# Between shared expert and routed experts: the tables, the zero rows and the first weights set up inside the shared expert's last chunk

## The reference: what is computed

```python
h = layernorm(x) * (1 + cb) + sb
scores = sigmoid(h @ router_weight.T)                 # 4096 tokens, 16 experts
idx = grouped top-2 of (scores + e_bias)              # 4 groups of 4, 2 groups kept
w = scores at idx, divided by their sum
routed = sum over the 2 chosen e: w_e * (relu2(h @ w_up[e]) @ w_down[e])   # 512 -> 256 -> 512
shared = relu2(h @ shared_up) @ shared_down                                # 512 -> 1024 -> 512
out = x + gb * (routed + shared)
```

## Time and profile before

| | before |
|---|---|
| time, median of 3 runs | 2291.51 us (2287.38 to 2297.24) |
| the profiled execution: its own time | 2298.3 us |
| its span in the trace | 2296.4 us |
| PE busy | 1909.7 us, 83% |
| DVE busy | 1264.3 us, 55% |
| ACT busy | 822.5 us, 36% |
| POOL busy | 687.5 us, 30% |
| shared stage's last chunk, from PE's first up matmul's relu to the last add | about 1809 to 1855 us of the span |

### The profile page before, as it was taken

The page is one execution under the profiler, slowest core; times in us unless marked ns, Lnnn a source line. Parts: engine busy times, 40 slices in busy tenths (PEclk is TensorE's granted clock), DMA queues, the critical chain, the costliest instruction groups (busy, mean ns, idle before and its releaser), DMA issues. The chain is left out here.

```text
span 2296.4 us, 34896 instructions
## 1 busy us (share of the span) xinstructions
PE 1909.7 (83%) x9947; PEld 1197.6 (52%) x9948; DVE 1264.3 (55%) x3069; ACT 822.5 (36%) x1372; POOL 687.5 (30%) x775
## 2 busy tenths in 40 slices
PE   4789989899899999899899885999999928999900
PEld 0645434644435644436544433777777727888800
DVE  3356657345566355573565627555555336575558
ACT  1335445245453254452344522222222104545400
POOL 0101116001124011143011243445545569260064
PEclk8789999899999899999899996999999969999955
DMA  6221131222312222404112314222222157554388
GB/s 217 60 45 36 42 101 61 61 56 56 75 37 67 54 56 56 111 6 115 29 38 45 74 65 143 92 87 91 87 91 88 70 193 258 189 183 153 135 307 319
DMA packets 104960, 232.37 MB, mean 101 GB/s; under 512 B 20440, under 2 KB 20440, under 8 KB 104812
## 3 DMA queue, kind: packets, MB, share of 16 engines
q1 hardware_dynamic: 81008, 171.86, 25.8%
q0 software_dynamic: 14848, 50.34, 6.3%
q10 hardware_dynamic: 8960, 8.41, 1.2%
HBM read 113.06 MB, written 67.17 MB: 78 GB/s over the span
## 5 line engine op out<-in xcount | busy, mean ns | idle before, releaser
L400 ACT ACTIVATE pr<-sc 128x1024 f32<-128x1024 f32 (+3 forms) x384 | 308.1, 811 | 320.1 <-PE sc L669 286.0
L324 POOL TENSOR_SCALAR_AFFINE_SELECT pr<-pr 128x256 f32<-128x256 f32 x256 | 105.7, 413 | 1008.8 <-ACT pr L400 1008.6
L689 PE MATMUL O<-pr,V 128*32 128x512 f32 (+3 forms) x3072 | 339.7, 518 | 13.3 <-ACT oD L412 13.2
L513 DVE TENSOR_REDUCE mx<-ring 128x1 f32<-128x512 f32 x256 | 169.6, 679 | 282.7 <-PE ring L644 281.6
L509 DVE CUSTOM_DVE_ANT_0 ring<-ring,mask 128x512 f32<-128x512 f32 (+3 forms) x512 | 240.9, 512 | 81.0 <-PE ring L644 80.0
L669 PE MATMUL sc<-stk 128*128 128x512 f32 (+3 forms) x768 | 251.6, 410 | 19.6 <-ACT pr L400 17.6
L669 PEld LDWEIGHTS sc<-stk 128*128 128x128 f32 x768 | 120.4, 196 | 268.0 <-ACT pr L400 154.0
L644 PE MATMUL ring<-stk 96*128 96x512 f32 (+3 forms) x768 | 225.5, 393 | 39.0 <-DMA stk<-st 28.5
L644 PEld LDWEIGHTS ring<-stk 96*128 96x128 f32 x768 | 147.6, 208 | 92.0 <-issue 25.0
L538 DVE RECIPROCAL oD<-oD 128x128 f32<-128x128 f32 x128 | 117.7, 935 | 32.9 <-ACT oD L412 32.9
L635 PE MATMUL ring<-hhi,whi 128*128 128x512 f32 x256 | 111.4, 435 | 27.2 <-DVE hlo L488 15.2
(11 more groups left out here) (246 smaller groups left out, 3776.5 us busy)
## 6 DMA issues: line engine op xcount, KB each, us to landing
stk<-st SPq DMA_DIRECT2D x192, 256.0 KB, 5.1
x_e<-xs SPq DMA_DIRECT2D x79, 256.0 KB, 2.6
ys<-y_e SPq DMA_DIRECT2D x79, 256.0 KB, 2.0
xt<-in_L_attn_x_dram ACTq DMA_DIRECT2D x16, 512.0 KB, 5.5
st<-in_L_attn_x_dram SPq DMA_DIRECT2D x32, 256.0 KB, 2.7
x1d<-pr SPq DMA_DIRECT2D x32, 256.0 KB, 2.0
xb<-x1d SPq DMA_DIRECT2D x32, 256.0 KB, 3.0
part<-y_sh SPq DMA_DIRECT2D x32, 256.0 KB, 2.0
```

The costliest lines, as they stand in the source:

```text
L324: nc.gpsimd.affine_select(out=t, in_=t, compare_op=ALU.is_ge, fill=0.0, base=0, pattern=[[0, 2], [1, P]], channel_multiplier=-1).then_inc( ...
L400: nc.scalar.activation(pr[:, g % PRB, :, off:], sc[g % 2][:, :, off:], ACT.Exp, scale=SCALE).then_inc(exp_done, 1)
L513: nc.vector.tensor_reduce(mx[:, heads[0]:heads[-1] + 1, qt, part], bank[:, 0:len(heads) * w].rearrange("p (e k) -> p e k", e=len(heads)), ...
L689: last = nc.tensor.matmul(O[row:row + 32, off:], V[:, col:col + DH], pr[:, g % PRB, e, off:], start=(i == 0), stop=(i == 4 * c + 3))
```

## The change

What stood at the start of `expert_phase` moves into the last chunk of `shared_phase` (`b is None`). DVE makes the tables in four pieces behind the squares of blocks 2 to 5 (`count_tiles`, `place_tiles`, `find_tiles`, `list_tiles`), and copies them and works out `K.rows` between the second and the third `scaled` (`copy_tables`, `move_rows`). PE's three small transposes stand behind `down(q, 0)`. SP issues the 16 zero-row DMAs ahead of the last chunk's four stores, and waits for them at the end of the stage. POOL fetches experts 0, 1 and 2 ahead of its low parts 1, 2 and 3; ahead of its first two adds it splits experts 0 and 1, and ahead of the other two it fetches experts 3 and 4. `expert_phase` starts with the loads of x and with expert 2's split. The new tensors lie in memory that is dead by then: the weight slots over `uphi`, `uplo` and the other parity's `xb` and `h2`, the raw buffers over `dn_own` and the other parity's half of `turned`, which now holds `thi` and `tlo` together; the tables' scratch is `bc[:, 0]`. The iotas move to the start of the shared stage.

```diff
+def fetch_weights(nc, K, e): ...
+def split_high(nc, K, e): ...
+def split_low(nc, K, e): ...
-        xb = sb("xb", [P, 2, TPC, D])
-        h2 = sb("h2", [P, 2, TPC, D])
+        xb, h2 = [None, None], [None, None]
+        for par in range(2):
+            xb[par], h2[par] = sb(f"xb{par}", [P, TPC, D]), sb(f"h2_{par}", [P, TPC, D])
+        ahi = sb("ahi", [P, FC, CH], f32r)
+        alo = sb("alo", [P, FC, CH], f32r)
+        dn_own = sb("dn_own", [P, FC - 2, D])
+        turned = sb("turned", [P, 2, 2, KC, CH], f32r)
+        thi, tlo = turned[:, :, 0, :, :], turned[:, :, 1, :, :]
...
 # SP, chunk
+                if not more and q == NCH - 1:
+                    sp.wait_ge(pads_known, 1)
+                    for e in range(E):
+                        row = sp.value_load(K.padi[0:1, e:e + 1], min_val=e * REGION, max_val=e * REGION + T)
+                        sp.dma_start(K.xs[bass.ds(row, P), :], zero[:, :]).then_inc(padded, 16)
...
             sp.wait_ge(zero_out, 16)
+            sp.wait_ge(padded, 16 * E)
...
 # POOL, chunk
                 for m in range(FC):
+                    if b is None and 1 <= m <= RAW:
+                        fetch_weights(nc, K, m - 1)
                     low(q, m)
...
                 for j in range(TPC):
+                    if b is None and j < EARLY:
+                        pool.wait_ge(K.raw_in[j], 32)
+                        split_high(nc, K, j)
+                        split_low(nc, K, j)
+                    if b is None and EARLY <= j < 2 * EARLY:
+                        pool.wait_ge(K.w_ready, 2 * (j - EARLY) + 2)
+                        fetch_weights(nc, K, j - EARLY + RAW)
...
 # DVE, chunk
+                    if b is None and m == 2:
+                        count_tiles()
+                    if b is None and m == 3:
+                        place_tiles()
+                    if b is None and m == 4:
+                        find_tiles()
+                    if b is None and m == 5:
+                        list_tiles()
...
                 scaled(q, par, 1)
+                if b is None:
+                    copy_tables()
+                    move_rows()
                 scaled(q, par, 2)
...
 # PE, chunk
+                else:
+                    pe.wait_ge(in_columns, 1)
+                    for n in range(3):
+                        last = nc.tensor.transpose(tp[0][0:1, n, 0:NET], rowf[0:NET, 2 + n:3 + n], K.ident[0:NET, 0:NET])
+                    last.then_inc(in_rows, 1)
                 down(q, 1, range(FC // 2))
...
+EARLY = 2
...
 # expert_phase, SP
-            sp.wait_ge(tables, 1)
-            sp.wait_ge(zeroed, 1)
-            for e in range(E):
-                row = sp.value_load(padi[0:1, e:e + 1], min_val=e * REGION, max_val=e * REGION + T)
-                sp.dma_start(K.xs[bass.ds(row, P), :], zero[:, :]).then_inc(padded, 16)
-            sp.wait_ge(padded, 16 * E)
...
 # expert_phase, POOL
-            for e in range(RAW):
-                fetch(e)
-            for e in range(E):
-                if e == WR:
-                    pool.wait_ge(tables, 1)
-                split(e)
-                if e + RAW < E:
-                    pool.wait_ge(w_ready, 2 * e + 2)
-                    fetch(e + RAW)
+            for e in range(EARLY, E):
+                pool.wait_ge(K.raw_in[e % RAW], (e // RAW + 1) * 32)
+                split_high(nc, K, e)
+                split_low(nc, K, e)
+                if e + RAW < E:
+                    pool.wait_ge(K.w_ready, 2 * e + 2)
+                    fetch_weights(nc, K, e + RAW)
```

More of the change, by code:

```diff
@@ L843, in shared_phase @@
         y_out = [sem(f"y_out{i}") for i in range(2)]
+        K.rwhi = sb("rwhi", [P, KC, E], f32r)
+        K.rwlo = sb("rwlo", [P, KC, E], f32r)
+        K.ebias = sb("ebias", [P, E])
+        K.order = sb("order", [P, E])
+        K.region = sb("region", [P, E])
+        K.gtri = sb("gtri", [P, NG, NG])
+        K.tri = sb("tri", [P, P], bf16)
+        K.ones = sb("ones", [P, P], bf16)
+        kf, jf, ef = sb("kf", [P, NTILE]), sb("jf", [P, 1]), sb("ef", [P, E])
+        k_i, j_i, e_i = (sq[:, 0, at:at + n].bitcast(mybir.dt.int32) for at, n in ((0, NTILE), (NTILE, 1), (2 * NTILE, E)))
+        scratch = bc[:, 0, :, :].rearrange("p a d -> p (a d)")
+        more = scratch[:, 0:E * NTILE].rearrange("p (e k) -> p e k", k=NTILE)
+        mine = scratch[:, 0:2 * NTILE * E].rearrange("p (n e) -> p n e", e=E)
+        own = scratch[:, 2 * NTILE * E:]
+        ntile, ones_e, ends, starts, base, inside, other, padf, order_e, shift, rowf = (own[:, n * E:(n + 1) * E] for n in range(11))
+        moved = own[:, 11 * E:11 * E + 2 * NTILE]
         rw_raw = relu[0:E, 0, :]
         zero = sb("zero", [P, D])
-        dn_own = sb("dn_own", [P, FC - 2, D])
-        up_raw = [(slice(0, 2), xb[:, 1, :, :].rearrange("p j d -> p (j d)").rearrange("p (k n) -> p k n", k=2)),
-                  (slice(2, 4), h2[:, 1, :, :].rearrange("p j d -> p (j d)").rearrange("p (k n) -> p k n", k=2))]
+        up_raw = [(slice(0, 2), xb[1][:, :, :].rearrange("p j d -> p (j d)").rearrange("p (k n) -> p k n", k=2)),
+                  (slice(2, 4), h2[1][:, :, :].rearrange("p j d -> p (j d)").rearrange("p (k n) -> p k n", k=2))]
         dn_raw = [(slice(0, FC - 2), dn_own[:, :, :]), (slice(FC - 2, FC), y[:, :, :])]
@@ new lines, in place_tiles, with find_tiles @@
+            def place_tiles():
+                table(nc.vector.tensor_tensor_scan(ends, ones_e, ntile, 0.0, ALU.mult, ALU.add))
+                table(tt(starts, ends, ntile, ALU.subtract))
+                table(ts(base, starts, -float(P), -float(DUMMY), ALU.mult, ALU.add))
+                table(nc.vector.scalar_tensor_tensor(base, ef[:, :], float(REGION), base, ALU.mult, ALU.add))
+                nc.vector.tensor_scalar(K.endi[:, :], ends, float(PRIMED), None, ALU.add)
+            def find_tiles():
+                ts(inside, starts, jf[:, 0:1], None, ALU.is_le)
+                table(ts(other, ends, jf[:, 0:1], None, ALU.is_le))
+                table(tt(inside, inside, other, ALU.subtract))
+                red(rowf[:, 2:3], other, AX.X, ALU.add)
+                table(red(rowf[:, 0:1], inside, AX.X, ALU.add))
+                table(ts(rowf[:, 2:3], rowf[:, 2:3], float(E - 1), None, ALU.min))
+                table(tt(other, inside, base, ALU.mult))
@@ L1197, in transposes @@
                 for k in range(KC):
-                    last = nc.tensor.transpose(tp[j % 2][:, k, :], h2[:, par, j, k * P:(k + 1) * P], K.ident[:, :])
+                    last = nc.tensor.transpose(tp[j % 2][:, k, :], h2[par][:, j, k * P:(k + 1) * P], K.ident[:, :])
                 last.then_inc(t_done, 1)
@@ L1535, in _ @@
-            nc.vector.tensor_copy(jf[:, :], j_i[:, :])
-            then(nc.vector.tensor_copy(ef[:, :], e_i[:, :]))
-            then(tt(more[:, :, :], K.count[:, :].unsqueeze(2).broadcast_to([P, E, NTILE]),
-                    kf[:, :].unsqueeze(1).broadcast_to([P, E, NTILE]), ALU.is_gt))
-            then(red(ntile[:, :], more[:, :, :], AX.X, ALU.add))
-            then(nc.vector.tensor_tensor_scan(ends[:, :], ones[:, :], ntile[:, :], 0.0, ALU.mult, ALU.add))
-            then(tt(starts[:, :], ends[:, :], ntile[:, :], ALU.subtract))
@@ L1551, in _ @@
-            ts(inside[:, :], starts[:, :], jf[:, 0:1], None, ALU.is_le)
-            then(ts(other[:, :], ends[:, :], jf[:, 0:1], None, ALU.is_le))
-            then(tt(inside[:, :], inside[:, :], other[:, :], ALU.subtract))
-            red(rowf[:, 2:3], other[:, :], AX.X, ALU.add)
-            then(red(rowf[:, 0:1], inside[:, :], AX.X, ALU.add))
-            then(ts(rowf[:, 2:3], rowf[:, 2:3], float(E - 1), None, ALU.min))
-            then(tt(other[:, :], inside[:, :], base[:, :], ALU.mult))
@@ L1586, in _ @@
         def _(pe):
-            pe.wait_ge(in_columns, 1)
-            for n in range(3):
-                last = nc.tensor.transpose(txb[0][0:1, n, 0:NET], rowf[0:NET, 2 + n:3 + n], K.ident[0:NET, 0:NET])
-            last.then_inc(in_rows, 1)
-            pe.wait_ge(tables, 1)
             slot = {}
```

209 lines of the change are left out of this document (98 added, 111 removed).

## The result

| | before | changed |
|---|---|---|
| time, median of 4 runs each, on one chip | 2294.38 us (2287.38 to 2301.44) | 2263.79 us (2255.4 to 2272.2) |
| ratio, with its 95% interval | | 0.9867 [0.9817, 0.9916] |
| the profiled execution's span | 2296.4 us | 2253.5 us |

What follows compares the result with a forecast made beforehand. PE's standstill between barrier and restart, 38.1 us, was taken as the passage to shorten. -33.0 + 6.8 = -26.2 us from the 2291.5 us median gave 2265 us; likeliest range 2259 to 2271, with the worse tail 2257 to 2274.

Steps and rivals of the forecast that it cites:

- The restart: Barrier to PE's restart: 5.1 us instead of 38.1, with 4.1 us for the load's landing; -33.0 us.
- The shared stage with its barrier: Shared stage's end: POOL's added work in the last chunk makes the last add end near 1862.0, +6.8 us.
- POOL's tail: Last chunk: two splits, four adds and two fetches take 22.3 us, plus 1.5 us lost to DVE.
- The sends' end: Last chunk: low part 7 and the sends end perhaps 0.5 us later, 1838.2 instead of 1837.7.
- The chunks ahead: Shared stage before the last chunk: iotas and three copies at its start cost under 0.5 us, taken as 0.
- Add to barrier: Last add to barrier: stores come back within some 3 us; no added time counted.
- PE's down product: Last chunk: later by low part 7's 0.5 us plus about 0.6 us for three transposes, its end covered.
- The tables on DVE cost 0: Last chunk: squares may be late by 1 to 2 us, covered by POOL's lateness; cost 0, uncovered at most 2 us.
- Behind the restart: Expert stage: POOL has expert 3 split with 11 us to spare before tile 7 asks; taken as 0.

Runs made afterwards that it cites:

- b_zeros_late: Changed kernel, but SP stores the 16 rows of zeros behind the barrier again; 2293.13 us, ratio 0.9986 to the kernel before.
- a_layout: Kernel before with only the changed kernel's memory layout, no instruction moved; 2293.85 us, ratio 0.9994 to the kernel before.
- b_fetch_late: Changed kernel, but experts 3 and 4 are fetched behind the barrier; 2265.16 us, ratio 0.9868 to the kernel before.
- a_after: The changed kernel again, unchanged; 2266.24 us, ratio 0.9879 to the kernel before.
- c_best: Changed kernel, experts 0 and 1 split on ACT and DVE, experts 3 and 4 fetched earlier, row table later, sends behind low part 7; 2257.37 us, ratio 0.9819.
- d_final: c_best with three sends between low parts, five behind low part 7, experts 3 and 4 fetched behind the second add; 2257.82 us, ratio 0.9820 to before.
- b_no_weights: Changed kernel, but POOL fetches and splits no weights in the last chunk; 2268.75 us, ratio 0.9876 to the kernel before.
- a_before: The kernel before again, unchanged; 2295.86 us, ratio 0.9995 to itself.
- a_shift: Kernel before with only five small unused tensors put in front of the shared stage's memory; 2293.62 us, ratio 0.9989 to the kernel before.

## Why the prediction was right, and where only its sum was

**The restart, forecast -33.0 us, measured -34.8 us.** Barrier to restart went from 38.06 to 3.27 us. SP's first load is issued 0.8 us behind the barrier (1858.54, 1859.32), and PE starts 2.5 us after that. I had taken 4.1 us for this landing from the earlier trace rows; that load went out right behind 16 stores, and the median of the earlier trace rows, 2.6 us, was the better guide. b_zeros_late shows the mechanism: with the zeros back, the gain is gone.

**The shared stage with its barrier, forecast +6.8 us, measured +7.2 us (483.4 to 490.7), from other parts than I said.**
- POOL's tail from the last send to the last add: two splits, four adds and two fetches. Forecast 22.3 + 1.5 = 23.8 us; it took 23.5 us (from 1826.20, the last send's end, to 1848.39 + 1.28). Before it was 17.45 us. Of that, DVE cost 1.9 us (3.25 and 3.38 instead of 2.35 each), forecast 1.5.
- The sends' end: forecast 0.5 us late, measured 1.5 us, from the chunk's first `relu` (28.8 us before, 30.3 us now).
- The chunks ahead: the last one began 3.6 us earlier in the stage (at 431.65 and 428.05 us), which I had at zero. It lasts: in all ten profiles with the changed chunk it began at 425.0 to 428.2 us, in the four without it at 431.5 to 431.8. The layout's shorter blocks, 0.4 us in each of seven chunks, would be 2.8 us of it, but a_layout is one of the four, so what else is needed is open.
- Add to barrier: assumed unchanged at 5.57 us, measured 8.87 and 9.63 us. This step failed. I had reckoned the stores' landing "within some 3 us" and thought only of POOL's time for the fetches, not of their bytes ahead of the last stores. b_fetch_late shows it for 2.3 of the 3.3 us: 6.53 us without them.

So the forecast was 0 + 0.5 + 6.3 + 0 = 6.8, and the trace has -3.6 + 1.5 + 6.0 + 3.3 = 7.2. The two terms that I had at zero nearly cancel. That this sum came out right is therefore luck, not a forecast of its parts. Counted from the stage's start, the last add is 3.9 us later, not 6.8.

**"PE's down product ... its end is covered by what follows."** It was covered, but its size was wrong. I had put the low parts 0.5 us late. PE, with the clock in the stretches under the rows:

```profile
1820.15 0.50 PE L1414 MATMUL dn<-dnhi,ahi 128*128 128x512 f32 x1 [0.70 <-POOL alo L988]
1820.72 0.40 PE L1414 MATMUL dn<-dnhi,alo 128*128 128x512 f32 x1
1823.83 0.79 PE L1414 MATMUL dn<-dnhi,ahi 128*128 128x512 f32 x1 [2.71 <-POOL alo L988]
1824.43 0.63 PE L1414 MATMUL dn<-dnlo,ahi 128*128 128x512 f32 x1
1824.85 0.63 PE L1414 MATMUL dn<-dnhi,alo 128*128 128x512 f32 x1
...
1820.00:1822.00 2.00, 0.97 (x3) 0.48 (x3) 0.00 (x0) 0.00 (x0) 1.55 (x3) 1.00 1.02 395
1822.00:1824.00 2.00, 0.17 (x1) 0.17 (x2) 0.00 (x0) 0.00 (x0) 1.81 (x3) 0.66 1.01 383
1824.00:1826.00 2.00, 2.00 (x7) 1.50 (x8) 0.48 (x1) 0.00 (x0) 1.70 (x2) 0.50 0.88 335
1826.00:1828.00 2.00, 2.00 (x6) 1.52 (x6) 0.21 (x1) 0.00 (x0) 1.99 (x3) 0.50 0.91 344
1828.00:1830.00 2.00, 2.00 (x7) 1.59 (x6) 0.00 (x0) 0.00 (x0) 1.92 (x2) 0.64 0.72 270
1830.00:1832.00 2.00, 2.00 (x10) 1.68 (x9) 0.00 (x0) 0.00 (x0) 2.00 (x2) 1.00 0.25 93
```

PE waited 0.70 and 2.71 us for low parts 6 and 7, where before one wait of 1.40 us stood. Over the second its clock fell from 1.00 to 0.50, that is from 2.4 to 1.2 GHz, and from 1823.83 until 1829.2 its matmuls came 0.43 us apart instead of 0.227: 12 matmuls and three transposes, 5.7 us where some 3.1 would do, so 2.6 us. The last chunk took 48.1 us instead of 44.15 (48.4 in a_after): 2.0 from the waits, 2.6 from the clock, 0.3 to 0.6 from the transposes, less 1.3 us for 192 matmuls at the shorter pitch. It costs nothing in the changed kernel, since POOL's tail ends later still (5.7 us behind PE), but it is what c_best and d_final gain: there the down product waits for no low part, the clock is 1.00 throughout, and the last chunk takes 41.5 and 41.8 us.

**"The tables on DVE cost 0; a square may be late by 1 to 2 us."** The delays of 1 to 2 us did come, but they added up from piece to piece, and POOL, held up as well, was no cover. A square starts 0.6 us behind its `relu` in the kernel before; in the changed one those of blocks 3 to 6 start 2.5, 2.4, 4.2 and 4.7 us behind. The `relu` and the square of block 6, then rows in which POOL and DVE lengthen each other:

```profile
1812.69 0.60 ACT L1081 ACTIVATE relu<-up 128x512 f32<-128x512 f32 x1 [1.60 <-PE up L1399]
1817.38 1.29 DVE L1283 TENSOR_TENSOR sq<-relu 128x512 f32<-128x512 f32 x2
...
1805.74 1.31 POOL L988 TENSOR_TENSOR alo<-sq,ahi 128x512 fp32r<-128x512 f32 x1
1807.24 1.38 POOL L993 DMA_INDIRECT xs<-h,slotu  x1 [0.18 <-issue]
1814.24 1.48 POOL L993 DMA_INDIRECT xs<-h,slotu  x1 [0.18 <-issue]
...
1803.08 1.78 DVE L1217 TENSOR_TENSOR bc<-count,kf 128x512 f32<-128x512 f32 x1
1805.90 1.20 DVE L1222 CAST padi<-bc 128x16 int32<-128x16 f32 x1
1808.46 1.32 DVE L1231 TENSOR_SCALAR endi<-bc 128x16 int32<-128x16 f32 x1
1812.42 1.69 DVE L1242 TENSOR_TENSOR bc<-bc 128x16 f32<-128x16 f32 x1
```

Sends take 1.38 and 1.48 us, where one in the clear takes 0.98; `bc<-count,kf` takes 1.78 us, the same instruction 0.69 in the kernel before; and small instructions of 16 elements 1.20, 1.32 and 1.69 us, where others of this shape take 0.17. The fetches are not the whole cause: b_no_weights has none and PE still waits 2.28 us. Nor do tables and fetches suffice: c_best and d_final keep both, have fewer sends ahead of low part 7, and PE doesn't wait, though in d_final squares are up to 2.7 us late. So the wait grows with what stands in POOL's queue: 1.40 us with the sends alone (before), 2.28 us with the tables beside them, 3.4 us in two waits with the fetches too, and none with three sends (d_final) or no send (c_best) ahead of low part 7. No run has the fetches without the tables, so what each is worth by itself isn't shown. The Trainium skill (SBUF — State Buffer, section SBUF: two separate sides) has GpSimd and VectorE take a shared port in turn, each for a whole instruction, where VectorE's runs in a two-port mode or reads two inputs from SBUF. The trace agrees: the cast `padi<-bc`, with one input, ends 0.05 us behind POOL's low part (1805.90 + 1.20, 1805.74 + 1.31); whether it ran in such a mode no row shows. The same section warns that a DMA issued by GpSimd starves while VectorE runs in a two-port mode. Here the fetches show nothing of it: their issues took 0.70 to 0.84 us, as in the kernel before, and over all 16 experts they landed after 4.4 to 8.0 us (4.3 to 9.3 us before). Two indirect sends did grow, by 0.4 and 0.5 us.

**Behind the restart, forecast 0.** Right: no wait for POOL stands in the first ten tiles. The expert stage is 2.2 us shorter in one profile and 0.9 us in the other; a_layout and a_shift have 0.8 and 1.0 less as well, so I take it for chance, which isn't shown.

**Why 2265 was met.** The sum of the touched stages fell by 29.8 us in the profile and 30.4 us between a_before and a_after, against 26.2 forecast. The 1.8 us of the landing and the expert stage's 1 to 2 us make up the difference.

## What to carry to other kernels

Before work is moved ahead of a barrier, ask which of its parts the first waiting load depends on: here 16 small stores were 27 us of the path, and the weights, the bulk of what was moved, gave back ahead of the barrier most of what they saved behind it (9 to 12 of 13 us). Count a moved DMA's bytes against the next store or load that somebody waits for, not only its issue. And put what an engine must still deliver to PE ahead of everything in its queue that nobody waits for yet.
